# Cross-attention and a top-2 expert layer on one core: each expert's weights loaded to `homes` in one transfer or in two chained ones

## What is computed

```python
# x: (64, 128, 256), context: (64, 128, 192); 16 heads of 64; 8 experts, top 2, hidden 512
x = x + attention(layernorm(x), context) @ w_o + b_o
g = softmax(layernorm(x) @ gate)                      # over 8 experts
gate_topk = top-2 of g, others 0, divided by its sum
h = relu(einsum('btd,edh->beth', layernorm(x), W1) + b1)
y = einsum('beth,ehd->betd', h, W2) + b2
out = x + einsum('bte,betd->btd', gate_topk, y)
```

## Time and profile before

| | |
|---|---|
| median of 3 runs | 1687.49 us (1686.41 to 1689.08) |
| the profiled execution | 1682.29 us, its span 1680.6 us |
| busy in the span | TensorE 97%, weight loads 92%, DVE 75%, ACT 72%, POOL 48% |
| TensorE's mean granted clock | 0.992 |
| 8 loads of `homes` | 2048 KB each, 8.7 to 13.7 us to landing, median 9.6 |
| chain that ended last | TensorE 92%, DMA 3% |

### The profile page before, as it was taken

One profiled execution on the slowest core, in us unless ns is written; L12 is line 12 of the kernel. 1 busy time (PEld: TensorE's weight loads), 2 busy tenths in 40 slices (PEclk: granted clock), 3 DMA queues, 4 the chain that ended last, 5 costly groups with the idle time before them and its releaser, 6 DMA issues.

```text
span 1680.6 us, 45384 instructions
## 1 busy us (share of the span) xinstructions
PE 1636.9 (97%) x13932; PEld 1554.1 (92%) x13933; DVE 1252.0 (75%) x3302; ACT 1218.4 (72%) x3547; POOL 802.9 (48%) x887
## 2 busy tenths in 40 slices
PE   6999999999999999999999999999898999999997
PEld 5899999999999999999999999999798999999997
DVE  5777777777777777777777777777777777777775
ACT  5777777777777777777777777777565677677774
POOL 3335444444444444444444444444346555555555
PEclk9999999999999999999999999999899999999999
DMA  7121111122111112221111222111489655555554
GB/s 237 47 64 64 57 57 57 57 87 73 64 59 57 57 57 77 78 66 62 57 57 57 66 81 73 63 57 45 134 266 283 124 87 87 86 89 86 84 88 60
DMA packets 105752, 142.91 MB, mean 85 GB/s; under 512 B 12464, under 2 KB 88368, under 8 KB 105584
## 3 DMA queue, kind: packets, MB, share of 16 engines
q1 hardware_dynamic: 59728, 86.88, 15.9%
q0 software_dynamic: 26672, 36.27, 12.4%
q10 hardware_dynamic: 19312, 19.27, 4.3%
HBM read 75.00 MB, written 67.38 MB: 85 GB/s over the span
## 4 chain that ended last, share of the span: by engine, by line
PE 92%; DMA 3%; DVE 1%; POOL 1%; issue 1%; ACT 0%; SPq 0%; DVEq 0%; POOLq 0%; ACTq 0%
PE bank_a L1259 38%; PE bank_s L1259 16%; PE bank_t L1266 8%; PE bank_v L1292 8%; PE bank_t L1259 5%; PE bank_v L1259 5%; PE bank_a L1322 2%; PE bank_a L1323 2%; DMA out<-stage_room,number 2%; PE bank_a L1331 2%; PE bank_a L1330 2%; PE bank_a L1406 2%; PE bank_a L1348 1%; PE bank_a L1305 1%; PE bank_a L1343 1%
## 5 line engine op out<-in xcount | busy, mean ns | idle before, releaser
L597 POOL TENSOR_TENSOR prob<-prob,inv 128x512 f32<-128x512 f32 x256 | 269.0, 1051 | 624.9 <-DVE inv L882 624.8
L701 ACT ACTIVATE prob<-bank_s,low 128x128 f32<-128x128 f32 x1024 | 363.2, 368 | 146.3 <-DVE low L877 143.3
L877 DVE TENSOR_REDUCE low<-bank_s 128x4 f32<-128x512 f32 x256 | 176.5, 689 | 245.9 <-PE bank_s L1259 245.8
L662 POOL DMA_INDIRECT out<-stage_room,number x142 | 231.9, 1633 | 53.7 <-issue 53.6
L701 ACT ACTIVATION_READ_ACCUMULATOR prob<-bank_s,low 128x1 f32 x1024 | 210.3, 205 | 0.0
L810 ACT ACTIVATE hidt_h<-hid 128x512 fp32r<-128x512 f32 x142 | 89.8, 633 | 118.8 <-DVE hid L1181 114.9
L905 DVE TENSOR_TENSOR kt_l<-bank_a,kt_h 64x512 fp32r<-64x512 f32 x256 | 173.1, 676 | 1.7
L1266 PE MATMUL bank_t<-ident,prob 128*128 128x128 f32 x1024 | 163.0, 282 | 9.2 <-POOL prob L597 9.2
L1259 PE MATMUL bank_s<-kt_l,qt_h 128*128 128x256 f32 x512 | 165.8, 324 | 0.0
L694 ACT ACTIVATE probt<-bank_t 128x512 f32<-128x512 f32 x256 | 152.8, 597 | 17.5 <-PE bank_t L1266 16.8
L739 ACT ACTIVATE ot_h<-bank_v 128x512 fp32r<-128x512 f32 x128 | 76.5, 598 | 120.2 <-PE bank_v L1292 119.5
(11 more groups left out here) (209 smaller groups left out, 5333.2 us busy)
## 6 DMA issues: line engine op xcount, KB each, us to landing
stage_room<-lists ACTq DMA_DIRECT2D x71, 265.0 KB, 2.9
halves<-stage_room SPq DMA_DIRECT2D x32, 512.0 KB, 3.8
homes<-halves SPq DMA_DIRECT2D x8, 2048.0 KB, 9.6
xin<-in_x SPq DMA_DIRECT2D x32, 256.0 KB
stage_room<-in_x SPq DMA_DIRECT2D x32, 256.0 KB, 3.1
stage_room<-in_w SPq DMA_DIRECT2D x32, 256.0 KB, 3.8
out<-stage_room SPq DMA_DIRECT2D x32, 256.0 KB, 2.2
cin<-in_ctx SPq DMA_DIRECT2D x32, 128.0 KB
```

Of the source, the lines that this page charges most:

```text
L597: pool.tensor_tensor(prob[:, n % 4, :, :], prob[:, n % 4, :, :], wide(inv[:, n % 4, :], P), ALU.mult).then_inc(s_norm.sem, 1)
L662: pool.indirect_dma_start(out, bass.IndirectOffsetOnAxis(ap=number[:, u, b:b + 1], axis=0), ysum[:, u, b, :], None, compute_op=ALU.add).th ...
L701: e = act.activation(prob[:, n % 4, h, :], bank_s[n % 2][:, h * P:(h + 1) * P], ACT.Exp, bias=low[:, n % 4, h:h + 1], scale=-1.0, accum_ou ...
L877: dve.tensor_reduce(low[:, n % 4, :], bank_s[n % 2][:, :].rearrange("p (h k) -> p h k", h=4), AX.X, ALU.min).then_inc(s_low.sem, 1)
```

## The change

`load_home` issues two transfers in place of one: quarters 0 and 1 of the expert (W1), then, when these have landed, quarters 2 and 3 (W2). SP itself waits between them. `arrived` waits for both, so the rest of the program sees an expert's weights when all of them are there, as before.

```diff
+                def load_half(e, k):
+
+                    many = QUARTERS // 2
+                    first = e * HOME + k * many * 2 * QUARTER
+                    sp.dma_start(homes[:, first:first + many * 2 * QUARTER].rearrange("p (u c) -> p u c", u=many),
+                                 halves[e * QUARTERS + k * many:e * QUARTERS + (k + 1) * many, :, :, :]
+                                 .rearrange("u p s c -> p u (s c)")).then_inc(home_in[e], 16)
+
                 def load_home(e):
-                    first = e * QUARTERS
-                    sp.dma_start(homes[:, e * HOME:(e + 1) * HOME].rearrange("p (u c) -> p u c", u=QUARTERS),
-                                 halves[first:first + QUARTERS, :, :, :].rearrange("u p s c -> p u (s c)")
-                                 ).then_inc(home_in[e], 16)
+                    load_half(e, 0)
+                    sp.wait_ge(home_in[e], 16)
+                    load_half(e, 1)
 
                 def arrived(e):
-                    sp.wait_ge(home_in[e], 16)
+                    sp.wait_ge(home_in[e], 32)
                     sp.sem_inc(at_home, 1)
```

## The result

The changed kernel took 1684.37 us (median of 14 runs, 1679.58 to 1687.87) beside 1688.22 us for the kernel before (14 runs, 1683.64 to 1691.14): a ratio of 0.9979, 95% interval 0.9971 to 0.9987, so 3.6 us faster by the ratio. I had forecast 7.0 us. Two later comparisons of the same two kernels gave 0.9959 (0.9945 to 0.9973) and 0.9969 (0.9958 to 0.9980), 6.9 and 5.2 us. The sign and the mechanism held. The size for the ordinary runs was forecast too large; the three comparisons average 5.2 us.

The account below looks back on a forecast made before the run. TensorE bounds the kernel, with one hole where the DMA engines are full; 2.4 + 2.8 + 2.3 - 0.5 = 7.0 us off the median 1687.49 gives 1680.5 us, 8-in-10 range 1675.5 to 1689.7.

Parts of the forecast that it names:

- The term for the longer crowd: Weight loading and pad stores after expert 0: crowd of 93 us instead of 75, 0.5 us set aside as loss.
- I take the same 7.0 us off: Whole kernel: the profiled gain applied to the runs' median, 1687.49 to 1680.5 us.
- The clock's part of the hole: TensorE's turn and up products after the 4.00 us wait: slow clock costs 2.3 us, all expected back.
- the hole of 9.7 us and its chain: TensorE, tiles 2 to 10: 9.7 us lost, 6.40 idle, through late adds, `tags(6)` and an x load of 11.31 us.
- Costs put at nothing: Later landing of expert 0, experts 1 to 7 (13.2 us each) and the pad stores: cost 0 each.
- They cost 8.6 us each and 4.1 at best; I expect 6.5: Three serial scatter-adds to `out`: faster adds end the `tags(6)` delay and TensorE's smaller waits, 2.4 us gained.
- the first three terms of the sum: Gains in the hole: adds 2.4 us, late x load 2.8 us, TensorE's clock 2.3 us.
- the 1.2 us that I let stay of the x load's wait: TensorE's 4.00 us wait: x load falls from 11.31 to 8.6 us, leaving 1.2 us, 2.8 gained.
- My allowance that ordinary runs hold a larger hole: Unprofiled runs, longer than the profiled one, may hold a larger hole: up to 12 us off allowed.
- fair shares: DMA queues already take turns, so halving loads changes almost nothing: 3 us off to 2 more, about 1687; chance 0.27.
- longer hole: Longer crowd costs more: 1689.7 us, or 1693.8 with one more late x load; chance 0.16.
- The estimate of 14 us of longer loading: Seven transfers added after 1221 us, at about 2.0 us fixed cost each, lengthen the loading by 14 us.

Follow-up runs that it names:

- experiment 3: Changed kernel with SP's wait between the two halves removed, both issued at once; ratio 0.9994 to the kernel before.
- 12: Expert 0's load alone in two chained halves, experts 1 to 7 in one transfer each as in the kernel before; ratio 1.0000 to the kernel before.
- experiments 6: Kernel before, with experts 1 to 7 loading W1 alone (1024 KB) and every tile using expert 0's W2; ratio 0.9967 to the kernel before.
- 11: Changed kernel, each half also waiting for two more tiles to be turned; ratio 0.9962 to the kernel before.
- experiments 2: Changed kernel run again with no edit; ratio 0.9959 to the kernel before.
- 8: Changed kernel run a third time with no edit; ratio 0.9969 to the kernel before.
- experiment 5: Kernel before, with each whole load issued before the previous one landed, two in flight; ratio 0.9993 to the kernel before.
- experiment 9: Weights in 512 KB quarters, each issued when the last but one has landed, two in flight; ratio 0.9970 to the kernel before.
- 7: Changed kernel with SP also waiting between the eight stores of pad; ratio 0.9965 to the kernel before.
- experiment 1: Kernel before run again with no edit; ratio 1.0005 to the kernel before.

## Why the prediction was right in kind and off in size

Two steps of the prediction failed. The term for the longer crowd was 0.5 us, and tiles 10 to 18 lost 2.4 us on average, 3.3 in the first profile. And the gain worked out from one trace was taken over for the ordinary runs, 7.0 us for 3.6 measured.

The clock's part of the hole shows in a window of the kernel before, right behind the wait of 4.00 us: granted clock 0.50. In the changed kernel it is 1.00 from 1235 to 1311 us.

```profile
1286.40:1289.00 2.60, 2.53 (x12) 2.54 (x13) 0.68 (x1) 0.78 (x2) 1.87 (x3) 0.50 0.62 157
```

- What bounds the kernel, the hole of 9.7 us and its chain (slow adds, `tags(6)`, a late x load, the lower clock behind it): right. The hole's total repeats in four profiles of kernels with whole loads or unchained halves (second stage 444.5 to 444.9 us), while its pieces move: in experiment 3 and 12 the x load's wait is 2.27 and 1.20 us and a second wait of `hidt_l` follows.
- Costs put at nothing (expert 0, experts 1 to 7, the stores of pad): right. 13.2 us per expert was forecast and measured.
- "They cost 8.6 us each and 4.1 at best; I expect 6.5": 7.0, 6.0 and 8.9 us in the first profile, 21.9 in sum, and 21.0 and 22.9 in the copies. The adds gained a little less than forecast, but 3 us in sum was all that `tags(6)` needed, and all waits of TensorE in tiles 6 to 9 are gone. In what the hole gives back the forecast was too careful. Tiles 2 to 9 took 50.1 us in the first profile and 50.0 and 49.8 in the copies, against 59.3 and 58.7 before: 9.0 us gained, where the first three terms of the sum made 7.5. Nothing of the 1.2 us that I let stay of the x load's wait did stay.
- "Against it stands the longer crowd, 93 us instead of 75: I set aside 0.5 us": the first step that failed. Tiles 10 to 18 lost 3.3, 2.1 and 1.7 us in the three profiles of the changed kernel, 2.4 on average, and the kernel before 0.0 and 0.2. The length of the crowd isn't the cause either (experiments 6 and 11). A loss of 1.2 to 2.7 us sits in tiles 8 to 15 once the hole is gone, with weights moving (experiments 2, 8, 11 and the first) or not (experiment 6, 2.4 us). Before, the hole stood just ahead of them and the other engines caught up in it; that is argued, no run shows it. In experiment 6 the chain of waits through these tiles goes through POOL's adds and DVE's `tags` and `bias2`, and DVE's table work lies in them; which of them holds it is open. The two errors nearly cancel: the second stage came out at 6.9 us less over three profiles, forecast 7.0. That agreement is luck.
- "I take the same 7.0 us off": the second step that failed. In the first comparison the runs gave 3.6 us, although the first two profiles differ by 5.9 us in the second stage; the other two gave 6.9 and 5.2 us. The second stage repeats within 2 us in profiles, while the runs of one kernel in one comparison scatter over 2 to 8 us; which stretch scatters, and why the first comparison gave least, stays open. My allowance that ordinary runs hold a larger hole has nothing for it: the hole's loss was the same in four profiles. The kernel before's profile lay 5.2 us under its median; a pace of 37.17 for 36.92 us makes 7 us and is the likelier reason, but the pace of unprofiled runs isn't on record.
- Rival "fair shares": its forecast of no change fell with experiments 2, 3 and 8. But experiment 5 shows it partly true: an add doesn't wait for all that stands ahead, it costs about 9 us beside 2048 or 4096 KB (the third add 10.2 us beside 4096). "DMA: Bandwidth & Descriptors" of the Trainium skill, section "Queues, rings and completion order", has the engines take turns by packets. By this rule alone chained quarters two at a time and whole loads, at nearly the same rate, should cost an add the same; experiment 9 (21.4 against 26.7 us) does not agree.
- Rival "longer hole": no further x load was late. It fell.
- The estimate of 14 us of longer loading, from the fixed cost in "DMA: Bandwidth & Descriptors" of the Trainium skill, section "Anatomy of one DMA": that section gives the cost for transfers that GpSimd issues, and these are SP's. Measured, the loading took 92.3 us instead of 75.0, 2.5 us for each of the seven added transfers, a little more than by the page and as the prediction's own sum had it.

What is shown: the gain comes from SP's wait between the parts (experiment 3), and the adds go with the bytes of weights in flight and not with their rate (experiment 9, one profile). 512 KB give 19.8 us of serial adds, 1024 KB 20.4 to 22.9 in six profiles with the queue kept busy (experiments 2, 6, 7, 8, 9 and the first), 2048 KB 26.2 to 27.0 in four, 4096 KB 28.3. Only the sums part so cleanly: single adds overlap, 5.4 to 8.7 us beside 1024 KB and 8.2 to 9.3 beside 2048. Why it is the bytes in flight and not the rate, inside the DMA engines, isn't shown.

## What to carry to other kernels

When a bulk load with slack shares the DMA engines with small transfers on the critical chain, keep few bytes of it in flight by waiting on the issuing queue between parts; the wait is what helps, and cutting the transfer without it gave nothing. Cost the load by its last consumer and the small ones by the bytes in flight beside them, and expect the gain to level off (here at 1024 KB; 512 KB and slower pacing gave no more): a smaller loss of another kind, whose cause is open here, remained in all of them. Before a profile's span is set against a median, compare the period of a long loop in both: 0.28 us in each iteration of a loop that nobody edited made 7 us, more than the whole effect.

## What the runs showed of the hardware

- The add of tile 0 or 1 (two indirect DMAs of 128 rows of 1 KB, from the second issue to the next `turn`) cost 4.2 us with no weights in flight, 5.4 to 8.7 us, 7.0 on average, with 1024 KB in flight (six profiles), 8.2 to 9.3, 8.8 on average, with 2048 KB (four), 8.9 and 9.1 with 4096 KB (one profile).
- Two whole loads in flight moved weights at 9.60 MB in 30 us instead of 6.29, with the three serial adds at 28.3 us instead of 26.2 to 27.0.
- The same attention loop ran at 36.92 us per iteration in one comparison and at 37.2 us in two others, each on another chip, with a granted clock of 1.00 from 600 to 900 us at either pace; all four kernels of a comparison agreed.
- Behind TensorE's waits of 4.00 us (the kernel before) and 3.75 us (experiment 1) the granted clock was 0.50, which is 1.2 of 2.4 GHz, for the next 2.6 and 2.3 us. In experiment 3 it was 0.68 from 1280 to 1285 us, behind a wait of 1.79 us, and 1.00 from 1291.8 to 1294 us, behind one of 2.27 us: the length of the one wait didn't decide it.
